# A graph network with two layers: the store of a block's counts asked for at the top of SyncE's turn

## The chip, the cores and the metric

The kernel runs on one core of a Trainium2 chip. The metric is the device time of one execution in microseconds (us). Five engines with instruction streams of their own take part: TensorE (PE, with its weight loads as PEld), VectorE (DVE), ScalarE (ACT), GpSimd (POOL) and SyncE (SP), which here only asks for DMAs. They meet at semaphores alone.

## What is computed

There are 6250 nodes with 128 features each and 200000 edges, sorted by the node they end at. Cut to what matters:

```python
h = x @ W + b_W;  xi, xj = split(h)
xji = (xj[src] + edge_attr @ W_e + b_We) / (in_degree[dst] + 1e-6)
x1 = layernorm(x + xi + segment_sum(xji, dst))
h2 = x1 @ W1                                 # with self loops and degree norm
out = segment_sum(h2[src] * norm, dst) + b1
y = leaky_relu(batchnorm(out) * gamma + beta)
result = layernorm(x1 + y)
```

## The kernel before

**Blocks and turns.** The nodes are worked through in 25 blocks of 256. For each block the kernel builds a table of counts (how many edges go from each source node to each node of the block) as products of one-hot matrices, 16 slots to a block. A sum over edges is then a matrix product with the table. Each engine runs a loop of turns `b` that are written out in full. In turn `b`, slot `s`, these are the steps that matter here:

- VectorE builds the one-hot matrices of two slots at a time (`one_hots`, L608 to L622), in a ring of six slots that TensorE's counting frees. At slot 2 it makes the keys of the next block (`make_keys`) and the edge keys of the one before (`edge_keys`, which need the loaded destinations).
- TensorE counts a slot (`count`, L852, products of L858), which waits until ScalarE has emptied the slot before the last (`pair_out` of slot s-2), for there are two buffers `pair_ps`. Then it does a fifteenth of the product of the block before with its table (`product`, L863, products of L876 and L884), and at two slots the sums of 4 streams of edge rows (`edges`, L895).
- ScalarE casts each counted slot into the table in SBUF (`pair_out`, L1056, cast of L1065). There are two tables, `counts[b % 2]`, so at slot 0 it first waits until the table of block b-2 is in HBM (L1061, semaphore `counts_kept`). At slot 10 it waits for a load of 64.5 KB of destinations, `rows_i`, and turns them into floats for block b+4 (`float_rows(b + 4)`, L1144 to L1153, called at L1183). Its instructions run in order, so whatever stands behind one of these waits is held up too.
- SyncE asks for DMAs (L398 to L425): the row load for block b+4 (`load_rows`, L299), eight register loads of start values (`start_values`, L325), the eight small loads of edge destinations (`load_destinations`, L330), the inverse degrees (`keep_inverse`), then the store of the counts of block b-1 (`keep_counts(b - 1)`, L346), which waits for the block's last cast, then early sums, four loads of 576 KB of edge rows (`load_edges(b, 0)`, L336), the store of finished rows (`keep_rows(b - 2)`, L357, which waits for ScalarE's slot 12), and four more loads of edge rows.

After the last block the tables are loaded again for the second layer (L426 to L441), and a last stage normalises and writes the rows.

**What sets the order around the change.** All of SyncE's DMAs go to one hardware queue, in the order in which its instructions stand. The store is 3136 KB for blocks 0 and 1 and gets smaller, down to 1600 KB, because part of a later block's table is used at once for the second layer and need not be kept. Blocks 23 and 24 are not stored.

Of the kernel before, what the change touches and what calls it, by code (L numbers as in the profile page):

```python
# [31 lines left out]
NB = -(-N // BN)  # L32
# [47 lines left out]
def slots(b):  # L80
    return SL if b < NB - 1 else LAST_SLOTS


def first_slot(b):
    return SL * b
# [6 lines left out]
def cols(b):  # L92
    return 2 * SW * slots(b)
# [15 lines left out]
def groups(b):  # L109
    return 2 if b < NB - 1 else -(-LAST // (EG * EC))  # L110
# [13 lines left out]
def early(k):  # L124
    return min(4 * max(0, k - 1), EARLY_MOST)
# [69 lines left out]
def layers(nc, block, x, src, dst, ea, W0, b0, We, be, keep, scratch):  # L195
    with ExitStack() as ctx:
# [102 lines left out]
        def load_rows(engine, b):  # L299
            reach(engine, S["rows_float"], b - ROW_RING + 1)  # L300
            engine.dma_start(rows_i[b % ROW_RING][:, :],
                             bass.AP(tensor=dst.tensor, offset=first_row(b), ap=[[HR, P], [1, HR + 1]]))\
                  .then_inc(rows_in[b % ROW_RING], 16)

        def load_late_rows(engine):
            engine.wait_ge(S["late_cleared"], 1)
            at = E - ROW_SPAN
            engine.dma_start(late_rows_i[0:P - 1, :],
                             bass.AP(tensor=dst.tensor, offset=at, ap=[[HR, P - 1], [1, HR + 1]])).then_inc(S["late_rows_in"], 16)
            engine.dma_start(late_rows_i[P - 1:P, 0:HR], dst[E - HR:E].rearrange("(o n) -> o n", o=1))\  # L310
                  .then_inc(S["late_rows_in"], 16)

        @block.sync
        def _(sp):
# [10 lines left out]
            def start_values(b):  # L325
                sp.wait_ge(S["starts_known"], b + 1)
                return [sp.value_load(estart_i[EP * c:EP * c + 1, b:b + 1], min_val=0, max_val=E - EE)
                        for c in range(groups(b) * EG)]

            def load_destinations(b, starts):  # L330
                reach(sp, S["e_keyed"], b - 1)
                for c in range(groups(b) * EG):
                    sp.dma_start(edst[b % 2][:, c, :], dst[bass.ds(starts[c], EE)].rearrange("(p j) -> p j", j=EJ))\
                      .then_inc(edst_in[b % 2], 16)

            def load_edges(b, g, starts):  # L336
                reach(sp, S["e_summed"], edge_group(b - 1, g) + 1)
                if b == 0 and g == 1:
                    sp.wait_ge(S["x_low"], len(X_PIECES))
                    sp.wait_ge(S["x_turned"], len(OWN))  # L340
                for c in range(EG):
                    sp.dma_start(ebuf[g][:, c, :, :].rearrange("p j f -> p (j f)"),
                                 ea[bass.ds(starts[g * EG + c], EE), :].rearrange("(p j) f -> p (j f)", j=EJ))\
                      .then_inc(e_in[g], 16)

            def keep_counts(k):  # L346
                sp.wait_ge(S["pair_out"], first_slot(k) + slots(k))
                at, n = early(k) // 2 * cols(k), HS * cols(k)
                sp.dma_start(scratch["counts"][k * P:(k + 1) * P, at:n], counts[k % 2][:, at:n])\
                  .then_inc(counts_kept[k % 2], 16)  # L350

            def keep_early(k):
                sp.wait_ge(S["early_out"], early_blocks(k + 1))
                n = cols(k)
                sp.dma_start(scratch["sz"][:, k * BN:k * BN + n], early_sum[k % 2][:, 0:n]).then_inc(early_kept[k % 2], 16)

            def keep_rows(u):  # L357
                sp.wait_ge(S["x1_ready"], u + 1)
                if u < NB - 1:
                    sp.dma_start(scratch["x1"][u * BN:u * BN + BN, :].rearrange("(p t) f -> p t f", t=2),  # L360
                                 x1[u % 2][:, :, :]).then_inc(x1_kept[u % 2], 16)
                    return
                for half in range(2):
                    sp.dma_start(scratch["x1"][u * BN:N, :].rearrange("(p t) f -> t p f", t=2)[half],
                                 x1[u % 2][64 * half:64 * half + LAST_P, 0, :]).then_inc(x1_kept[u % 2], 16)

            def keep_inverse(b):
                sp.wait_ge(S["shares_ready"], b + 1)
                n = P if b < NB - 1 else 64
                sp.dma_start(scratch["dinv"][b * BN:b * BN + 2 * n].rearrange("(p t) -> p t", t=2),  # L370
                             dinv[0:n, 2 * b:2 * b + 2]).then_inc(S["dinv_kept"], 16)

            def load_counts(i):
                b = AGAIN[i]
                at, n = early(b) // 2 * cols(b), HS * cols(b)
                if i < 4:
                    sp.wait_ge(S["e_summed"], edge_group(NB - 1, groups(NB - 1) - 1) + 1)
                else:
                    sp.wait_ge(S["z_gathered"], i - 3)
                sp.wait_ge(counts_kept[b % 2], 16 * (b // 2 + 1))  # L380
                sp.dma_start(again[AGAIN_AT[i % 4]][:, at:n], scratch["counts"][b * P:(b + 1) * P, at:n])\
                  .then_inc(counts_in[i % 4], 16)
# [14 lines left out]

            for b in range(NB + 2):  # L398
                u = b - 2
                if b + ROW_RING < LATE:  # L400
                    load_rows(sp, b + ROW_RING)
                if b + ROW_RING == LATE:
                    load_late_rows(sp)
                if b < NB:
                    starts = start_values(b)
                    load_destinations(b, starts)
                    keep_inverse(b)
                if 1 <= b <= NB - 2:
                    keep_counts(b - 1)
                if early(b - 2):  # L410
                    keep_early(b - 2)
                if b == NB:
                    sp.dma_start(w1[:, :], keep["W1"]).then_inc(S["vectors_in"], 16)
                    for k, a in enumerate(keep["vectors1"]):
                        sp.dma_start(vec[:, k:k + 1], a.rearrange("(p o) -> p o", o=1)).then_inc(S["vectors_in"], 16)
                    sp.wait_ge(S["dinv_kept"], 16 * NB)
                if b < NB:
                    load_edges(b, 0, starts)
                if 0 <= u < NB:
                    keep_rows(u)  # L420
                if b < NB and groups(b) > 1:
                    load_edges(b, 1, starts)
                if b == NB - 1:
                    load_counts(0)
                    load_counts(3)  # L425
# [425 lines left out]
        def _(pe):  # L851
# [111 lines left out]
            def turn_x(m):  # L963
                h, n = OWN[m]
                piece = [h < 2 * z for _, z in X_PIECES].index(True)
                last_piece = [h + n <= 2 * z for _, z in X_PIECES].index(True)
                for k in range(piece, last_piece + 1):
                    pe.wait_ge(S["x_in"][k], 16 * x_loads(k))
                pe.wait_ge(S["consts"], CONSTS)
                reach(pe, S["xT_out"], m - 1)  # L970
                for k in range(n):
                    last = nc.tensor.transpose(turn_ps[m % 2][:, k, :], xrows[:, h + k, :], ident[:, :])
                last.then_inc(S["x_turned"], 1)
# [832 lines left out]
```

## Time and profile before

| | before |
|---|---|
| median of 3 runs | 938.35 us (937.87 to 938.45) |
| the profiled execution, its own time | 936.68 us |
| its span, first to last instruction | 934.6 us |
| mean granted TensorE clock | 0.985 |
| busy: PE, DVE, ACT, POOL | 95%, 72%, 48%, 37% of the span |
| q1, SyncE's DMA queue | 239.46 MB, 73.7% of 16 engines' span |

The profile is one execution of the program. Times in its rows count from the first instruction. A row of the timeline gives the start, the length, the engine (SPq is SyncE's sequencer, which asks for DMAs), the line, the operation with what it writes and reads, how many instructions are merged, and in brackets the idle time of the engine before it with what ended it.

### The profile page before, as it was taken

Reading aid. Unit: us, or ns where it says so; the run is one execution under the profiler, and the core shown is the slowest. Engines: PE = TensorE matmul, PEld = TensorE weight load, DVE = VectorE, ACT = ScalarE, POOL = GpSimd, SP = SyncE. Lnnn points to the kernel's source line nnn. Section 1 sums busy time; section 2 is a strip of 40 time slices with the busy share of each in tenths; the row PEclk is TensorE's granted clock in tenths of the full one; section 3 lists DMA queues with packets and bytes.
Section 4 is the critical chain, followed back from the end, with each engine's and each line's share of the span. In section 5 each row is a group of like instructions: output and inputs, shape, how many; then the busy total and the mean of one; then the engine's idle time right before and its main releaser. Section 6 shows DMA issues by size and latency. Waiting matters only on the chain.

```text
span 934.6 us, 30500 instructions
## 1 busy us (share of the span) xinstructions
PE 883.9 (95%) x12210; PEld 791.2 (85%) x12210; DVE 676.6 (72%) x1249; ACT 450.3 (48%) x983; POOL 349.4 (37%) x401
## 2 busy tenths in 40 slices
PE   4867999999999999999999999999999999999995
PEld 4756888888988898989899999999988888888874
DVE  6999899999999998899888899888842111112255
ACT  3764666656666665556565556565542000000026
POOL 2236444455554444455334455434332011112200
PEclk8988999999999999999999999999999999999998
DMA  6428999998879788777878758678667897779654
GB/s 180 110 83 296 361 345 320 317 342 290 313 247 319 284 311 283 229 229 241 253 264 277 223 185 301 214 274 282 209 216 299 343 358 279 272 260 326 249 155 136
DMA packets 96762, 244.77 MB, mean 262 GB/s; under 512 B 39560, under 2 KB 64838, under 8 KB 90726
## 3 DMA queue, kind: packets, MB, share of 16 engines
q1 hardware_dynamic: 95014, 239.46, 73.7%
q0 software_dynamic: 1600, 3.28, 1.4%
q8 instruction: 100, 1.64, 0.8%
q14 instruction: 48, 0.39, 0.2%
HBM read 183.85 MB, written 58.85 MB: 260 GB/s over the span
## 4 chain that ended last, share of the span: by engine, by line
PE 85%; DVE 5%; issue 3%; ACT 3%; DMA 1%; SPq 1%; ACTq 0%; DVEq 0%
PE x_ps L876 26%; PE pair_ps L951 19%; PE pair_ps L858 13%; PE e_ps L895 10%; PE x_ps L884 9%; PE j_ps L933 2%; PE j_ps L981 2%; DVE lo_oh L616 1%; DVE key_oh L619 1%; PE pair_ps L960 1%; PE j_ps L934 1%; ACT counts L1065 1%; PE u_vps L1409 1%; DMA counts_kept<-counts 1%; DMA streams<-in_x 1%
## 5 line engine op out<-in xcount | busy, mean ns | idle before, releaser
L1065 ACT CAST counts<-pair_ps 128x784 bf16<-128x784 f32 x391 | 315.3, 817 | 251.5 <-PE pair_ps L858 244.1
L876 PE MATMUL x_ps<-counts,xsplit 128*128 128x256 bf16 (+1 forms) x2450 | 307.5, 271 | 0.0
L616 DVE TENSOR_TENSOR lo_oh<-counter,lo_t 128x2048 bf16<-128x2048 bf16 x196 | 252.3, 1287 | 53.9 <-PE pair_ps L858 52.5
L876 PEld LDWEIGHTS x_ps<-counts,xsplit 128*128 128x128 f16 x2450 | 222.1, 98 | 29.3 <-issue 7.1
L858 PE MATMUL pair_ps<-key_oh,lo_oh 128*128 128x100 bf16 x3128 | 207.8, 209 | 22.5 <-ACT counts L1065 15.4
L858 PEld LDWEIGHTS pair_ps<-key_oh,lo_oh 128*128 128x128 bf16 x3128 | 182.8, 98 | 36.9 <-issue 15.0
L619 DVE TENSOR_TENSOR key_oh<-counter,key_t 128x1600 bf16<-128x1600 bf16 x196 | 196.4, 1002 | 0.0
L895 PE MATMUL e_ps<-streams 128*32 128x128 f32 x3528 | 106.9, 274 | 0.1
L884 PE MATMUL x_ps<-counts,zown 128*128 128x256 bf16 (+1 forms) x840 | 105.9, 269 | 0.1
L951 PE MATMUL pair_ps<-streams,zown 128*128 128x256 bf16 x878 | 99.0, 273 | 0.0
L895 PEld LDWEIGHTS e_ps<-streams 128*32 128x32 f32 x3528 | 93.3, 110 | 4.8 <-issue 1.0
L476 POOL TENSOR_SCALAR quot<-deg 128x2 f32<-128x2 f32 x25 | 5.7, 226 | 243.2 <-DVE junk L595 231.5
L951 PEld LDWEIGHTS pair_ps<-streams,zown 128*128 128x128 f16 x878 | 85.8, 98 | 11.4 <-issue 0.2
L884 PEld LDWEIGHTS x_ps<-counts,zown 128*128 128x128 f16 x840 | 76.1, 97 | 10.3 <-issue 2.9
L492 POOL TENSOR_SCALAR bias<-linear,share 128x128 f32<-128x128 f32 x50 | 76.0, 1532 | 14.7 <-DVE vo L705 13.7
L951 PE MATMUL pair_ps<-counts,zown 128*128 128x256 bf16 (+1 forms) x732 | 79.9, 268 | 0.0
L951 PEld LDWEIGHTS pair_ps<-counts,zown 128*128 128x128 f16 x732 | 69.3, 98 | 9.2
L1313 ACT ACTIVATE u_co<-u_co 128x1 f32<-128x1 f32 x1 | 0.2, 203 | 156.0 <-DVEq L1351 156.0
L825 DVE TENSOR_TENSOR s_mem<-pair_ps,key_oh 128x256 f32<-128x256 f32 (+1 forms) x23 | 9.6, 418 | 83.8 <-PE pair_ps L951 81.3
L639 DVE TENSOR_TENSOR streams<-iota,ekeys 128x1152 f32<-128x1152 f32 x49 | 67.5, 1377 | 2.7 <-PE e_ps L895 0.3
L833 DVE TENSOR_TENSOR xsplit<-pair_ps,key_oh 128x256 f32<-128x256 f32 (+1 forms) x25 | 10.5, 419 | 58.7 <-PE pair_ps L960 57.0
L507 POOL TENSOR_TENSOR streams<-streams,key_oh 128x512 bf16<-128x512 bf16 x13 | 15.0, 1151 | 84.9 <-DMA streams<-counts_kept 84.9
(181 smaller groups left out, 890.6 us busy)
## 6 DMA issues: line engine op xcount, KB each, us to landing
streams<-in_edge_attr SPq DMA_DIRECT2D x196, 576.0 KB, 9.1
counts_kept<-counts SPq DMA_DIRECT2D x10, 1600.0 KB, 9.1
streams<-counts_kept SPq DMA_DIRECT2D x6, 1600.0 KB, 6.5
counts<-counts_kept SPq DMA_DIRECT2D x4, 1600.0 KB, 7.1
counts_kept<-counts SPq DMA_DIRECT2D x2, 3136.0 KB, 12.7
streams<-counts_kept SPq DMA_DIRECT2D x2, 3136.0 KB, 14.8
edst<-in_dst SPq DMA_DIRECT2D x196, 4.5 KB
streams<-in_x SPq DMA_DIRECT2D x3, 1024.0 KB, 5.7
```

What stands on the lines that cost most here:

```text
L492: last = g.tensor_scalar(bias[:, t, :], bje, share[:, 2 * b + t:2 * b + t + 1], None, ALU.mult)
L616: dv.tensor_tensor(lo_oh[:, ring, :, :, :].rearrange("p r w k t -> p (r w) k t"), counter[:, :, :].unsqueeze(1).to_broadcast([P, g, P, 2]) ...
L619: dv.tensor_tensor(key_oh[:, ring, :, :, :].rearrange("p r w k t -> p (r w) k t"), counter[:, 0:KW, :].unsqueeze(1).to_broadcast([P, g, KW ...
L639: dv.tensor_tensor(e_oh[g][:, :, :], iota[:, 0:EC].unsqueeze(1).to_broadcast([P, EG * EJ, EC]), ekeys[:, k].unsqueeze(2).to_broadcast([P, ...
L858: last = nc.tensor.matmul(pair_ps[at % 2][:, half_of, col:col + KW], lo_oh[:, at % RING, w // 2, :, w % 2], key_oh[:, at % RING, w // 2, : ...
L876: last = nc.tensor.matmul(x_ps[:, 0, 0:n], xsplit[:, q // 2, q % 2, :], by_hi[:, q // 2, :], start=(q == 0), stop=(q == 2 * HS - 1))
L884: last = nc.tensor.matmul(x_ps[:, 1, 0:n], zsplit[:, z // 2, z % 2, :], by_hi[:, z // 2, :], start=(z == 0), stop=(z == early(k) - 1))
L895: last = nc.tensor.matmul(e_ps[EC * c:EC * (c + 1), g, :], e_oh[g][:, c * EJ + j, :], ebuf[g][:, c, j, :], start=(j == 0), stop=(j == EJ - 1))
L933: nc.tensor.matmul(out, sx[:, t:m:2], wj, start=True, stop=False)
L951: last = nc.tensor.matmul(z_ps[i % 2][:, 0:n], zsplit[:, q // 2, q % 2, :], by_hi[:, q // 2, :], start=(q == early(b)), stop=(q == 2 * HS ...
L981: last = nc.tensor.matmul(j_ps[:, k, :], xT[m % 2][:, k, :], wi, start=True, stop=True)
L1065: a.copy(out.rearrange("p h (g n) -> p h g n", g=2), pair_ps[at % 2][:, :, 0:4 * KW].rearrange("p g (n h) -> p h g n", h=HI)[:, 0:HS]).the ...
```

## The change

One call is moved within SyncE's turn. Nothing is added or removed; the DMAs, their sizes and the semaphores stay the same.

```diff
             for b in range(NB + 2):
                 u = b - 2
+                if 1 <= b <= NB - 2:
+                    keep_counts(b - 1)
                 if b + ROW_RING < LATE:
                     load_rows(sp, b + ROW_RING)
                 if b + ROW_RING == LATE:
@@
                     starts = start_values(b)
                     load_destinations(b, starts)
                     keep_inverse(b)
-                if 1 <= b <= NB - 2:
-                    keep_counts(b - 1)
                 if early(b - 2):
                     keep_early(b - 2)
```

## Rows read from the trace of the kernel before

**Rows 1.** The page, part 1: busy time of TensorE.

```profile
PE 883.9 (95%) x12210; PEld 791.2 (85%) x12210; DVE 676.6 (72%) x1249; ACT 450.3 (48%) x983; POOL 349.4 (37%) x401
```

**Rows 2.** Waits of PE from 112 to 700 us: total, times, longest.

```profile
PE pair_ps L858 <- ACT counts L1065: 4.5, 11, 0.6
```

**Rows 3.** Timeline of ScalarE, 72.6 to 94.5 us (turn 1 into turn 2).

```profile
73.34 0.30 ACT L1151 ACTIVATE heads<-rows_i,shift 128x2 f32<-128x2 int32 x1
...
73.83 0.80 ACT L1065 CAST counts<-pair_ps 128x784 bf16<-128x784 f32 x1
...
81.69 0.49 ACT L1073 ACTIVATE sx<-x_ps,xscale 128x256 f32<-128x256 f32 x1
87.80 1.53 ACT L1065 CAST counts<-pair_ps 128x784 bf16<-128x784 f32 x2 [5.61 <-issue]
```

**Rows 4.** Timeline of SyncE, 63 to 90 us (its turn 1).

```profile
65.69 0.44 SPq L301 DMA_DIRECT2D rows_i<-in_dst  x1
71.10 3.85 SPq L333 DMA_DIRECT2D edst<-in_dst  x8
...
75.47 0.43 SPq L349 DMA_DIRECT2D counts_kept<-counts  x1
76.10 6.77 SPq L342 DMA_DIRECT2D streams<-in_edge_attr  x8
```

**Rows 5.** DMAs asked at 65.28, 65.69, 75.47, 76.10 us; last column: us to landing.

```profile
streams<-in_edge_attr SPq DMA_DIRECT2D x1, 576.0 KB, 7.7
rows_i<-in_dst SPq DMA_DIRECT2D x1, 64.5 KB, 7.5
...
counts_kept<-counts SPq DMA_DIRECT2D x1, 3136.0 KB, 12.3
...
streams<-in_edge_attr SPq DMA_DIRECT2D x1, 576.0 KB, 13.1
```

**Rows 6.** Timeline of PE, 77.6 to 95 us.

```profile
77.66 0.53 PE L858 MATMUL pair_ps<-key_oh,lo_oh 128*128 128x100 bf16 x8
...
78.79 0.53 PE L858 MATMUL pair_ps<-key_oh,lo_oh 128*128 128x100 bf16 x8
...
83.28 0.93 PE L876 MATMUL x_ps<-counts,xsplit 128*128 128x256 bf16 x7
88.75 0.83 PE L858 MATMUL pair_ps<-key_oh,lo_oh 128*128 128x100 bf16 x8 [4.55 <-ACT counts L1065]
...
93.88 0.93 PE L876 MATMUL x_ps<-counts,xsplit 128*128 128x256 bf16 x7
```

**Rows 7.** Busy time by stretch, 88 to 92 us: PE, PEld, DVE, ACT, POOL, PEclk, DMA, GB/s.

```profile
88.00:92.00 4.00, 3.25 (x27) 2.84 (x28) 3.92 (x8) 2.46 (x5) 2.37 (x5) 0.50 1.03 413
```

**Rows 8.** Timeline of ScalarE, 48 to 58 us: the last two casts of block 0.

```profile
51.66 1.53 ACT L1065 CAST counts<-pair_ps 128x784 bf16<-128x784 f32 x2
```

**Rows 9.** Timeline of ScalarE, 341 to 345 us: last cast of block 11.

```profile
341.98 0.81 ACT L1065 CAST counts<-pair_ps 128x784 bf16<-128x784 f32 x1 [0.60 <-PE pair_ps L858]
```

**Rows 10.** Timeline of SyncE, 338 to 356 us (its turn 12).

```profile
341.56 0.43 SPq L301 DMA_DIRECT2D rows_i<-in_dst  x1
...
353.80 0.43 SPq L349 DMA_DIRECT2D counts_kept<-counts  x1
```

**Rows 11.** Waits of SyncE's sequencer, whole span: total, times, longest.

```profile
SPq L360 <- ACT x_mem L1106: 167.2, 23, 9.3
```

**Rows 12.** Waits of DVE from 52 to 115 us: total, times, longest.

```profile
DVE lo_oh L616 <- PE pair_ps L858: 2.7, 3, 2.1
DVE row_junk L569 <- ACT lo_t L1090: 1.4, 1, 1.4
```

**Rows 13.** Busy time from 112 to 208 us, columns as in rows 7.

```profile
112.00:208.00 96.00, 92.31 (x1517) 82.83 (x1518) 94.43 (x168) 61.53 (x127) 50.77 (x56) 1.00 0.94 333
```

**Rows 14.** Timeline of ScalarE, 103 to 105 us: slot 10 of turn 2.

```profile
103.77 0.30 ACT L1151 ACTIVATE heads<-rows_i,shift 128x2 f32<-128x2 int32 x1
```

**Rows 15.** The page, part 6: the last ten stores of counts.

```profile
counts_kept<-counts SPq DMA_DIRECT2D x10, 1600.0 KB, 9.1
```

## The prediction

> **What bounds the kernel now.** I read the page's first part, then the waits of TensorE, then the chain around the first store. TensorE is busy for 95% of the span [rows 1]. From 112 to 700 us, which covers turns 3 to 24, its longest kind of wait adds up to 4.5 us in 11 waits of at most 0.6 us [rows 2]. So from turn 3 on nothing that SyncE does earlier can win anything, and whatever TensorE loses before 112 us stays lost. What matters lies in turns 1 and 2.
>
> There the timeline of ScalarE has one large hole: after the cast for the first product at 81.69 it sits idle for 5.61 us and casts slot 0 of block 2 only at 87.80 [rows 3]. The trace names no releaser ("issue"), but the code does: L1061 waits there for the store of block 0, whose table is to be overwritten. SyncE asked for that store at 75.47 [rows 4] and it landed 12.3 us later [rows 5], at 87.8. TensorE stood still for 4.55 us because of it [rows 6] and came back at a granted clock of 0.50, its 1.2 GHz level [rows 7]. This is the stall that the earlier store aims at.
>
> **The change, part by part.**
>
> *The store in turn 1 is asked for earlier.* SyncE is at the top of turn 1 at 65.69 [rows 4]. The last cast of block 0 ended at 51.66 + 1.53 = 53.2 [rows 8], so the moved wait costs nothing here and the store is asked for at 65.7 instead of 75.47.
>
> *When it lands.* The queue is not empty: the last of four edge loads was asked for at 65.28 and landed 7.7 us later, at 73.0; the row load, asked for next, landed at 65.69 + 7.5 = 73.2, just behind it [rows 5]. And an edge load asked for at 76.10, 0.6 us behind the store, took 13.1 us and landed at 89.2, which is 1.4 us after the store [rows 5]. So DMAs of this queue land in the order in which they were asked for. The store took 12.3 us from an empty queue. Some 2 us of that is start-up: 576 KB took 1.4 us behind other work, and 3136 KB at that pace are 7.8 us, but the store writes to HBM and may be slower. I take 10.3 us of service, near the row of the store itself, with 7.8 and 12.3 as ends. It then lands at 73.0 + 10.3 = 83.3 (80.8 to 85.3).
>
> *What is pushed behind it.* Moved past it are the row load, eight register reads, eight destination loads and the inverse degrees. The row load now stands behind 3136 KB. It lands 0.2 us behind the store, as it did behind the edge load, at 83.5 (81.0 to 85.5) instead of 73.2. ScalarE wants it in slot 10 of the same turn, at 73.34 [rows 3]: today it arrives just in time. So ScalarE will stand in `float_rows(5)` for 83.5 - 73.3 = 10.2 us, with the last five casts of turn 1 queued behind. The old stall of 5.61 us is gone (when slot 0 of block 2 comes, the store has landed), and a longer one stands in its place, some 8 us earlier.
>
> *What TensorE loses.* Its count of slot 13 needs the cast that follows the floats. Today that cast ends at 73.83 + 0.80 = 74.6 and the count starts at 77.66 [rows 3, 6], so 3.0 us of delay are free. After: floats at 83.5, cast from 84.0 to 84.8, count at 85.0. That is 85.0 - 77.66 = 7.3 us of delay. From there TensorE today needs until 83.28 + 0.93 = 84.2 to reach its hole, and leaves it at 88.75, 11.1 us after 77.66 [rows 6]. After, the same work without the hole takes 11.1 - 4.55 = 6.5 us, so that it is there at 91.5, which is 2.8 us later than 88.75.
>
> *The clock.* Today the work from 88.75 to 93.88 takes 5.1 us [rows 6]. At the pace of two counts 1.13 us apart (77.66, 78.79) it would take 2.9 with its three short key products, so the low clock [rows 7] costs 2.2 us. After, TensorE is idle longer, 7 us instead of 4.55, and comes back at 85.0, so the same cost falls due, and more of the slow stretch may be spent at work: between 0 and 1.6 us more (2.2 for 5.1 us, times the 3.7 us by which it starts earlier). I take 0.6.
>
> *Sum:* -4.55 (hole gone) + 7.3 (new hole) + 0.6 (clock) = +3.4 us, rounded. The ends of the landing (81.0 and 85.5) and of the clock give +0.3 to +6.4.
>
> *Can it be given back?* VectorE's ring is six slots. While TensorE stands, VectorE fills it and stands too, until slot 13 is counted at 85.5. In turn 2 it has 2.7 + 1.4 = 4.1 us of idle time today [rows 12], in which it catches up. From 112 to 208 us VectorE is busy for 94.4 of 96 us and TensorE for 92.3 [rows 13], and after that TensorE is the bound, so nothing returns the 3.4 us.
>
> *Turn 2.* The store of block 1 now waits for the last cast, at 83.5 + 8.4 = 91.9 or earlier (today 81.69 - 73.34 = 8.4 us hold all that is left of the turn [rows 3]). The row load follows it, where today it was asked for before. Ahead of both stand eight edge loads of 1.4 us, from 83.7 to about 95; the store to 105.6; the rows at 105.8. They are wanted at 103.77 + 3.4 = 107.2 [rows 14], with 3.0 us free behind that. No stall, with a margin of some 4 us.
>
> *Turns 3 to 23.* SyncE reaches the top of turn 12 at 341.56, and the block's last cast ends at 341.98 + 0.81 = 342.8 [rows 9, 10]. So the moved wait costs SyncE 1.2 us, the store is asked for some 11 us earlier than 353.80 [rows 10], and all that is moved behind it is a little over 1 us later. SyncE's own spare time covers that: it waits 167.2 us in 23 turns for finished rows [rows 11], 7.3 in each. The row load again stands behind a store, but this shrinks to 1600 KB, 9.1 us [rows 15]. Cost 0 while that cover lasts; if it goes, it is the third case below.
>
> The Trainium skill has a rule that speaks for another outcome. In "DMA: Bandwidth & Descriptors", section "Queues, rings and completion order", it says that descriptors of a ring are taken in order but without a barrier, so a later one may finish its write before an earlier one. By that rule the rows could overtake the store, and the sum would be that of the first rival instead of +3.4. The trace does not agree at this size: the edge load behind a store landed after it [rows 5].
>
> Against the runs: the profiled execution took 936.68 us, 1.67 less than the median of 938.35. I put the difference on the median: 938.35 + 3.4 = 941.8.
>
> **Rivals.**
>
> *1. Faster: the row load does not wait for the store.* Then only the old stall goes. VectorE then sets the pace of turn 2, which can shorten by VectorE's idle time at most, 4.1 us [rows 12]: 934.3. It decides if the rows land by about 76.2 (73.2 today and the 3.0 free). Against it stand the landings of rows 5; for it, that all of them are large loads or stand behind loads, except one. 0.13.
>
> *2. No change.* The two stalls weigh the same if the new one is 3 us shorter, with the rows landing at 80 to 81, for instance because the store's service is nearer 7.8 us. Or the clock comes back sooner. 938.4. The 12.3 us of the row speak against it. 0.13.
>
> *3. Slower still: the rows come late in later turns too.* From turn 2 to about turn 5 the stores are near 3 MB and stand behind edge loads. If gathers from GpSimd, which share the engines, push the landings 5 us past my reckoning, ScalarE stands in slot 10 again, at 1 to 2 us a turn: three turns, +4, so 945.8. 0.12.
>
> *The forecast*, one stall moved and made longer: 0.62.
>
> **How the numbers follow.** About 0.2% (1.9 us) is what a measurement of this kernel can tell from no change. Slower by more is the forecast (0.62, of which 0.03 falls short of 1.9 us) and rival 3: 0.62 - 0.03 + 0.12 = 0.71. Same: 0.13 + 0.03 = 0.16. Faster: 0.13. The forecast with its unknown costs spans 938.7 to 944.8. The range 938.0 to 945.0 holds it, some two thirds of rival 2 and a third of rival 3, about 0.75 to 0.8.
>
> **What would show it.** In turn 1 the store is asked for at 65.7 and the rows at 66.2, and these land near 83.5. ScalarE has an idle time of about 10 us ahead of the floats of L1151, ended by the row load, and none of 5.6 us ahead of the first cast of turn 2. TensorE has a hole of about 7 us from 77.8 to 85, with the clock at 0.50 behind it. In turn 12 the store is asked for within 2 us of the last cast. The prediction is wrong if the rows land before 80, if there is no idle time ahead of L1151 in turn 1, or if it comes back in turn 2 and later.

## The result, and the profile after

The change makes the kernel slower: 952.02 us against 938.11, medians of six runs each, a ratio of 1.0159 (95% interval 1.0118 to 1.02). That is 14 us, beyond the forecast's 941.8 and beyond its range. The runs of after spread over 10 us (948.86 to 958.99), those of before over 4. The profiled execution of after took 956.96 us, so its trace shows some 5 us more than the median.

The page of after, first the span, the busy times (against [rows 1]), then one of its DMA queues (packets, MB, share of 16 engines):

```profile
span 955.0 us, 30500 instructions
...
PE 890.3 (93%) x12210; PEld 794.6 (83%) x12210; DVE 677.7 (71%) x1249; ACT 450.9 (47%) x983; POOL 351.5 (37%) x401
...
q8 instruction: 100, 1.64, 0.7%
```

TensorE is busy for 6.4 us more with the same 12210 products, and the span is 20.4 us longer. The extra time is thus partly idle time, partly products that take longer.

**Where the 20.4 us lie.** I cut both traces at the end of the last cast of a block (ScalarE, L1065): a turn starts there. The table gives the length of each stretch in us.

| stretch | before | after | more |
|---|---|---|---|
| start to turn 1 | 53.2 | 54.9 | 1.7 |
| turns 1 and 2 | 58.8 | 62.9 | 4.1 |
| turns 3 to 10 | 204.4 | 217.0 | 12.6 |
| turns 11 to 23 | 361.9 | 363.9 | 2.0 |
| the rest | 256.4 | 256.3 | -0.1 |

The first row is no effect of the change: it lies ahead of the first moved store and reads 53.2 to 54.9 in all the kernels run here. Turns 1 and 2 are what the forecast spoke of. Turns 3 to 10 are where it put nothing.

**Turn 1.** The timeline of SyncE in after, against [rows 4]:

```profile
67.50 0.45 SPq L349 DMA_DIRECT2D counts_kept<-counts  x1
67.99 0.47 SPq L301 DMA_DIRECT2D rows_i<-in_dst  x1
```

The timeline of ScalarE in after, against [rows 3]:

```profile
74.32 0.81 ACT L1065 CAST counts<-pair_ps 128x784 bf16<-128x784 f32 x1 [0.37 <-issue]
87.35 0.30 ACT L1151 ACTIVATE heads<-rows_i,shift 128x2 f32<-128x2 int32 x1 [12.22 <-DMA rows_i<-in_dst]
...
94.81 1.54 ACT L1065 CAST counts<-pair_ps 128x784 bf16<-128x784 f32 x2
```

And the timeline of TensorE in after, against [rows 6]:

```profile
78.59 0.92 PE L876 MATMUL x_ps<-counts,xsplit 128*128 128x256 bf16 x7
88.78 0.82 PE L858 MATMUL pair_ps<-key_oh,lo_oh 128*128 128x100 bf16 x8 [9.27 <-ACT counts L1065]
```

The row load was asked for behind the store and came 19.4 us later (67.99 to 87.35). ScalarE stood 12.22 us for it, and TensorE 9.27 us for ScalarE. The cast at 94.81, the first of block 2, has no idle time ahead of it: the 5.61 us of [rows 3] are gone, and more than twice as much stands a few us earlier.

**Turns 3 to 10.** Busy time by stretch for the same stretch of the program (3208 products in each), first of before, columns as in [rows 7]:

```profile
112.00:316.30 204.30, 198.93 (x3208) 179.80 (x3208) 196.00 (x357) 132.24 (x272) 101.55 (x112) 1.00 0.90 318
```

and of after:

```profile
117.80:334.80 217.00, 203.79 (x3208) 182.57 (x3208) 196.39 (x357) 132.59 (x273) 102.23 (x112) 0.98 0.88 293
```

TensorE's idle time grew from 204.3 - 198.9 = 5.4 us to 217.0 - 203.8 = 13.2, which is 7.8 more, and its busy time by 4.9 us, at a mean granted clock of 0.98 instead of 1.00. Together these are the 12.6 us. The waits of TensorE from 112 to 700 us say which idle time grew, against [rows 2] (total, times, longest):

```profile
PE pair_ps L858 <- issue: 5.1, 2, 3.5
PE pair_ps L858 <- ACT counts L1065: 4.7, 11, 0.6
PE e_ps L895 <- issue: 4.1, 5, 1.7
PE x_ps L884 <- issue: 1.1, 2, 0.9
```

The wait for ScalarE is the same (4.5 us before, 4.7 now). New are nine stops without a releaser, 10.3 us in all. In before this view has one line of that kind:

```profile
PE pair_ps L858 <- issue: 1.2, 1, 1.2
```

**What these stops are.** The longest one, in the timeline of TensorE of after:

```profile
217.40 0.48 PE L858 MATMUL pair_ps<-key_oh,lo_oh 128*128 128x100 bf16 x7
221.33 0.22 PE L858 MATMUL pair_ps<-key_oh,lo_oh 128*128 128x100 bf16 x1 [3.45 <-issue]
```

and the one of before:

```profile
205.72 0.48 PE L858 MATMUL pair_ps<-key_oh,lo_oh 128*128 128x100 bf16 x7
207.45 0.22 PE L858 MATMUL pair_ps<-key_oh,lo_oh 128*128 128x100 bf16 x1 [1.24 <-issue]
```

It is the same place in both: between the seventh and the eighth product of one slot's eight, where the program has no wait at all. So TensorE did not wait for data. Now the products between one stop of after and the next, as busy time by stretch of TensorE alone (length, busy, number of products, granted clock, DMA share, GB/s); each stretch begins and ends at the first product behind a stop:

```profile
128.37:168.74 40.37, 38.49 (x623) 1.00 0.98 303
168.74:193.74 25.00, 24.12 (x373) 0.93 0.88 315
193.74:204.79 11.05, 9.66 (x121) 1.00 0.99 332
204.79:221.33 16.54, 13.09 (x252) 1.00 0.85 266
221.33:289.18 67.85, 65.89 (x993) 0.97 0.86 293
289.18:305.00 15.82, 14.94 (x252) 1.00 0.72 211
305.00:566.12 261.12, 258.44 (x3982) 1.00 0.81 259
```

The counts are 5, 3, 1, 2, 8, 2 and 32 times a number between 121 and 126; the longest gives 3982 / 32 = 124.4. The stops lie on a grid of 124.4 products, or, as each product has a weight load, of some 249 instructions. And the page's queue q8, whose kind is "instruction", moved 1.64 MB in 100 packets of 16.4 KB: 24420 instructions of TensorE / 100 = 244 in each. So a stop falls where one 16 KB packet of TensorE's own program ends and the next has to be there. The DMA view of after for three stretches around the stop of 3.45 us (packets, MB, share of 16 engines), in order: 210 to 219, 219 to 220, 220 to 221.3 us:

```profile
q1 hardware_dynamic: 1317, 1.56, 73.3%
...
q1 hardware_dynamic: 75, 0.32, 92.5%
q8 instruction: 1, 0.02, 6.1%
...
q1 hardware_dynamic: 131, 0.54, 103.1%
```

For nine us no packet of instructions came; one came between 219 and 220, and the product ran at 221.33. The same view, taken from each stop of after to the next, has 5, 3, 1, 2, 8, 2 and 32 packets of q8, one for each step of the grid. Here are the stretches 221.33 to 289.18 and 305.00 to 566.12:

```profile
q8 instruction: 8, 0.13, 0.7%
...
q8 instruction: 32, 0.52, 0.8%
```

It holds for all the kernels below too: the thirteen traces have 51 such stops from 112 to 700 us, and ahead of 50 of them a packet of q8 had landed 1.2 to 1.6 us before the product ran. In ten of the thirteen the same product, the one at 221.33 in after and at 207.45 in before, stands behind a stop.

Two of the stops are paid twice, for the clock falls behind them:

```profile
170.00:174.00 4.00, 3.83 (x23) 3.25 (x24) 4.00 (x6) 2.34 (x5) 3.75 (x4) 0.59 1.02 418
222.00:226.00 4.00, 4.00 (x33) 3.29 (x32) 2.54 (x5) 2.96 (x8) 0.00 (x0) 0.58 0.49 136
```

Behind the stops of 1.66 us (at 168.74) and of 3.45 us (at 221.33) TensorE runs mostly at the 1.2 GHz level. The length of a stop alone does not decide it: behind the one of 1.75 us that ends at 128.38 the clock stays at 1.00 (first line of the stretches above). The stretches between stops show it as 0.93 over 25.0 us and 0.97 over 67.85, which is some 1.75 + 2.0 = 3.8 of the 4.9 us of longer products.

The Trainium skill describes this traffic in "Runtime: NRT & Kernel Launch", section "Instruction fetch mechanics": an engine's instructions are refilled in blocks of 16 KiB, 256 instructions, over a DMA queue that the sequencer drives itself, and the cost of crossing a block is mostly hidden. The trace agrees on the block (249 counted, besides those that the count of products and weight loads leaves out). It agrees on "mostly hidden" for before, with 1.2 us between 112 and 700 us, and not for after, with 10.3.

**What fills the engines there.** The busy share of the 16 DMA engines in turn 3, in 40 slices of 0.7 us, 112 to 140 us of before:

```profile
DMA  9999999999999646790109939994959999999999
```

and 117.8 to 146 us of after:

```profile
DMA  9999899989999999799789999399276999999999
```

In before SyncE asks for the store at 122.22, as the edge loads of the turn before come to their end, and the engines have slices of 0 and 1 in the middle of the turn. In after it asks at 117.95, the store follows those edge loads at once, and most of the gap is filled. An estimate, which places the first product of each 16 KB block by counting products between the stops, shows the packets falling back: in turns 3 to 10 a packet begins to move, on average, 3.3 us after TensorE has entered the block ahead of it in before, and 4.8 us after that in after. The stop that ends at 128.38 lies 10 us behind this store; the one that ends at 168.74 lies 10 us behind the first of the turn's next edge loads, asked for at 158.63.

### The profile page after: what moved, and what is told of

It is laid out like the page before. It is cut to its first block, busy times and chain, and to the rows that moved or that the text cites. A ratio compares the mean times of both kernels' runs of the same rounds, so it can differ in the third digit from the quotient of the medians.

```text
span 955.0 us, 30500 instructions
## 1 busy us (share of the span) xinstructions
PE 890.3 (93%) x12210; PEld 794.6 (83%) x12210; DVE 677.7 (71%) x1249; ACT 450.9 (47%) x983; POOL 351.5 (37%) x401
## 3 DMA queue, kind: packets, MB, share of 16 engines
q8 instruction: 100, 1.64, 0.7%
## 4 chain that ended last, share of the span: by engine, by line
PE 87%; issue 3%; DVE 3%; ACT 3%; DMA 3%; SPq 0%; ACTq 0%; DVEq 0%
PE x_ps L876 26%; PE pair_ps L951 18%; PE pair_ps L858 14%; PE e_ps L895 11%; PE x_ps L884 9%; DMA rows_i<-in_dst 2%; PE j_ps L933 2%; PE j_ps L981 2%; PE j_ps L934 1%; ACT counts L1065 1%; PE pair_ps L960 1%; PE u_vps L1409 1%; DMA streams<-in_x 1%; ACT u_xo L1328 1%; PE e_ps L903 1%
## 5 line engine op out<-in xcount | busy, mean ns | idle before, releaser
L1065 ACT CAST counts<-pair_ps 128x784 bf16<-128x784 f32 x391 | 314.7, 817 | 256.9 <-PE pair_ps L858 249.7
L619 DVE TENSOR_TENSOR key_oh<-counter,key_t 128x1600 bf16<-128x1600 bf16 x196 | 198.7, 1014 | 0.0
L895 PE MATMUL e_ps<-streams 128*32 128x128 f32 x3528 | 109.0, 274 | 4.2 <-issue 4.1
L895 PEld LDWEIGHTS e_ps<-streams 128*32 128x32 f32 x3528 | 94.0, 110 | 10.2 <-issue 6.4
L492 POOL TENSOR_SCALAR bias<-linear,share 128x128 f32<-128x128 f32 x50 | 73.2, 1475 | 14.6 <-DVE vo L705 13.7
L833 DVE TENSOR_TENSOR xsplit<-pair_ps,key_oh 128x256 f32<-128x256 f32 (+1 forms) x25 | 10.5, 419 | 58.8 <-PE pair_ps L960 56.9
```

The costliest lines, as they stand in the source:

```text
L492: last = g.tensor_scalar(bias[:, t, :], bje, share[:, 2 * b + t:2 * b + t + 1], None, ALU.mult)
L619: dv.tensor_tensor(key_oh[:, ring, :, :, :].rearrange("p r w k t -> p (r w) k t"), counter[:, 0:KW, :].unsqueeze(1).to_broadcast([P, g, KW ...
L895: last = nc.tensor.matmul(e_ps[EC * c:EC * (c + 1), g, :], e_oh[g][:, c * EJ + j, :], ebuf[g][:, c, j, :], start=(j == 0), stop=(j == EJ - 1))
L1065: a.copy(out.rearrange("p h (g n) -> p h g n", g=2), pair_ps[at % 2][:, :, 0:4 * KW].rearrange("p g (n h) -> p h g n", h=HI)[:, 0:HS]).the ...
```

## The experiments

Eleven runs, of ten kernels, were made in four batches, each beside runs of the kernel before on the same chip (medians 937.05, 937.37, 937.68 and 938.41 us). A ratio is to the runs of before in the same batch. Theory A puts the whole loss on turn 1: the row load behind the store. Theory B says that turn 1 costs what was forecast, and that the rest is lost in the later turns by the early store as such.

**Turn 1 alone.**

```diff
+                if b == 1:
+                    keep_counts(b - 1)
                 if b + ROW_RING < LATE:
                     load_rows(sp, b + ROW_RING)
...
-                if 1 <= b <= NB - 2:
+                if 2 <= b <= NB - 2:
                     keep_counts(b - 1)
```

> Only the store of block 0 (turn 1) is asked for at the top of the turn; the stores of turns 2 to 23 stay where they were. Theory A (the row load waits behind the store, and that is the whole cost): ScalarE stands some 12 us ahead of the floats of turn 1 and the time is that of the change, 949 to 953. Theory B (the row load in turn 1 costs 4 to 5 us; the rest is TensorE running out of instructions in turns 3 to 10, because its instruction loads compete with a store that now runs while the first edge sums eat instructions fastest): the same hole in turn 1, but no idle times inside groups of products later, and 942 to 943.

Measured: 942.22 us, 1.0051 (1.0033 to 1.0069). Theory A falls. ScalarE's timeline has the forecast's stall:

```profile
82.81 0.30 ACT L1153 ACTIVATE heads<-rows_i,shift 128x2 f32<-128x2 int32 x1 [8.90 <-DMA rows_i<-in_dst]
```

So the mechanism that was forecast costs 5.2 us (3.1 to 6.5 by the interval), and not 14.

**All but turns 1 and 2.**

```diff
+                if 3 <= b <= NB - 2:
+                    keep_counts(b - 1)
                 if b + ROW_RING < LATE:
...
-                if 1 <= b <= NB - 2:
+                if 1 <= b <= 2:
                     keep_counts(b - 1)
```

> The stores of turns 3 to 23 are asked for at the top, those of turns 1 and 2 where they were. Theory A: no hole in turn 1 and so no cost, 937 to 939. Theory B: turn 1 as before, but TensorE stops inside groups of products in turns 3 to 10 with nothing to wait for, 8 to 10 us with the low clock behind it: 945 to 948.

Measured: 947.79 us, 1.0126 (1.0089 to 1.0163), in the range of theory B. But its trace shows two things at work, and so the number agrees in part by luck. The row load is late in two later turns, by 2.28 us at 185.51 and most in turn 3 (timeline of ScalarE):

```profile
134.22 0.30 ACT L1153 ACTIVATE heads<-rows_i,shift 128x2 f32<-128x2 int32 x1 [6.22 <-DMA rows_i<-in_dst]
```

and the waits of TensorE from 112 to 700 us hold the wait for ScalarE that follows from it, with the longer stops beside it:

```profile
PE pair_ps L860 <- ACT counts L1067: 7.6, 11, 3.3
PE e_ps L897 <- issue: 1.7, 3, 0.8
PE x_ps L886 <- issue: 1.3, 1, 1.3
```

The stops come to 3.6 us in six, not to the 8 to 10 expected. The wait of 3.3 us is the one in turn 3, and behind it the clock is at 0.50 from 135.65 to 141 us. Turns 3 to 10 are 8.6 us longer than in before, and the larger part of that is the late row load and this clock. So this run does not tell the two causes apart; the next pair does.

**The row load out of the way, in all turns and in turn 1.** In the first kernel the store stays at the top of every turn but behind the row load; in the second this is done in turn 1 alone, and the other stores are where they stood before.

```diff
                 if b + ROW_RING == LATE:
                     load_late_rows(sp)
+                if 1 <= b <= NB - 2:
+                    keep_counts(b - 1)
                 if b < NB:
...
-                if 1 <= b <= NB - 2:
-                    keep_counts(b - 1)
```

> The store stands at the top of every turn but behind the row load, so that the rows don't wait for it. Theory A: the hole in turn 1 goes, the old one of 5.6 us in turn 2 shrinks to 1 or 2 us, and the time falls to about 934, below the kernel before. Theory B: the same in turns 1 and 2, but the stops of turns 3 to 10 stay: 934 + 9, 940 to 946.

```diff
+                if b == 1:
+                    keep_counts(b - 1)
                 if b < NB:
...
-                if 1 <= b <= NB - 2:
+                if 2 <= b <= NB - 2:
                     keep_counts(b - 1)
```

> Only the store of turn 1 is moved up, to a place behind the row load; all others as before. Both theories: the stall of 5.6 us at the start of turn 2 shrinks to 1 or 2 us, with no hole in turn 1 and no stops later: about 934, faster than the kernel before by 0.4%.

Measured: 946.15 us, 1.0099 (1.0063 to 1.0135), and 935.68 us, 0.9986 (0.9971 to 1.0001). They differ only in the early stores of turns 2 to 23, and these cost 10.5 us though no row load stands behind one. From turn 3 to turn 23 the profiled executions differ by 11.1 us: 7.6 of idle time of TensorE and 3.5 of longer products. The waits of TensorE in the first, from 112 to 700 us, have 8.7 us of stops in seven where the second has 1.5 in one:

```profile
PE x_ps L876 <- issue: 2.6, 1, 2.6
PE e_ps L895 <- issue: 2.3, 2, 1.4
PE pair_ps L858 <- issue: 2.2, 2, 2.1
...
PE x_ps L884 <- issue: 1.6, 2, 0.9
```

In the second, ScalarE's old stall of 5.61 us [rows 3] shrank to 3.46 us, not to the 1 to 2 that I had reckoned, and the rows came in time:

```profile
75.35 0.30 ACT L1153 ACTIVATE heads<-rows_i,shift 128x2 f32<-128x2 int32 x1 [0.39 <-DMA rows_i<-in_dst]
...
87.25 2.34 ACT L1067 CAST counts<-pair_ps 128x784 bf16<-128x784 f32 x3 [3.46 <-issue]
```

Part of the gain is given back in the turns that follow. VectorE waits for a gather, and TensorE from 112 to 700 us waits for VectorE (waits of VectorE from 52 to 115 us, then of TensorE):

```profile
DVE bit_i L584 <- DMA gsrc<-in_src,start_i: 2.3, 1, 2.3
...
PE pair_ps L860 <- DVE key_oh L621: 1.6, 2, 0.9
PE pair_ps L860 <- issue: 1.5, 1, 1.5
```

The stops of the first lie on the grid of after. Its products between three of its stops (columns as above), and the timeline of its stop at 208.81:

```profile
183.58:208.82 25.24, 22.49 (x374) 1.00 0.96 317
208.80:276.14 67.34, 65.47 (x994) 0.97 0.88 294
...
208.81 0.22 PE L858 MATMUL pair_ps<-key_oh,lo_oh 128*128 128x100 bf16 x1 [2.07 <-issue]
```

374 is what lies between 193.74 and 221.33 in after (121 + 252), 994 what lies between 221.33 and 289.18, give or take a product at the ends. Another kernel, other times, the same places in the program: a wait for a load of data would move with the loads.

**Is it the size of a store's pieces or the amount that is under way?** Two forms of theory B. B1: the store's 25 KB rows hold up whatever comes behind them in a DMA engine, and smaller rows would help. B2: it is the unbroken backlog of store and edge loads. The first kernel below is the one with the row load first and each store asked for as four DMAs of a quarter of the columns (and the waits for stores counted accordingly). The second is the same kernel as it was, but the first four edge loads of a turn, from block 2 on, bring one of nine rows in each partition; the rest of those edge rows is left out.

```diff
+                part = (n - at) // 4
+                for q in range(at, n, part):
+                    sp.dma_start(scratch["counts"][k * P:(k + 1) * P, q:q + part], counts[k % 2][:, q:q + part])\
+                      .then_inc(counts_kept[k % 2], 16)
```

> As e3_rows_first, but each store is asked for in four DMAs of a quarter of its columns, so that a row of a partition goes in pieces of 6.3 KB and less instead of 25 KB. Theory B1 (TensorE's instruction load is held up by the large pieces of the store in its DMA engine): the stops of turns 2 to 10 mostly go, 935 to 939. Theory B2 (it is held up by whatever transfer is in flight while it is wanted, whatever the size of its pieces): no change against e3, 944 to 948.

```diff
+                if b >= 2 and g == 0:
+                    for c in range(EG):
+                        sp.dma_start(ebuf[g][:, c, 0, :],
+                                     ea[bass.ds(starts[g * EG + c], EE), :].rearrange("(p j) f -> p (j f)", j=EJ)[:, 0:F])\
+                          .then_inc(e_in[g], 16)
+                    return
```

> As e3_rows_first, but from turn 2 on each of the first four edge loads of a turn brings one of nine rows (64 KB instead of 576 KB); the other eight rows are left out, so that after the store, when TensorE's second burst of edge products comes, nothing large is in flight. Theory B2: the stops near the second burst (20 to 25 us after the turn's start) go, those near the first burst (8 to 10 us, store in flight) stay: 938 to 942. Theory B1: the store is what counts, so it stays at 943 to 948. Theory A': it is not the instruction loads but something that the move does to ScalarE or SyncE: unchanged, 944 to 948.

Measured: 943.91 us, 1.0074 (1.0047 to 1.0101), and 939.75 us, 1.0021 (1.0008 to 1.0034). The first interval overlaps that of the undivided store (1.0063 to 1.0135): B1 is not supported, but a part of it is not excluded, for the trace of the divided store, its fastest run, has 4.5 us of stops in five where the undivided store has 8.7. The second takes away most of the loss, as B2 said. Theory A', that the move does something to ScalarE or SyncE, gave 944 to 948 for the second and is out. In the trace of the second (936.6 us, the fastest of its ten runs) two stops are left from 112 us on, each some 8 us behind the store of its turn (asked for at 111.88 and 136.22), which is still under way; those in the second burst of edge loads are gone (timeline of TensorE):

```profile
120.91 0.43 PE L901 MATMUL e_ps<-streams 128*32 128x128 f32 x8 [0.93 <-issue]
...
145.65 1.06 PE L901 MATMUL e_ps<-streams 128*32 128x128 f32 x27 [1.15 <-issue]
```

The control has the same small edge loads with the stores of turns 2 to 23 in their old place:

```diff
+                if b == 1:
+                    keep_counts(b - 1)
...
-                if 1 <= b <= NB - 2:
+                if 2 <= b <= NB - 2:
```

> The control for e6_small_edges: the same small first edge loads from turn 2 on (one of nine rows, the other eight left out), but the stores of turns 2 to 23 in their old place, as in e4_turn1_rows_first. Theory B2: the one stop of 1.5 us that e4 still has near a second burst goes too, since nothing large is behind the store then: 933 to 936. Against e6 it is faster by the stops of the first burst, 2 to 4 us. If the small loads win time in another way, it is below 932.

Measured: 937.02 us, 1.0 (0.9985 to 1.0014), a us above what I had expected; its trace keeps two stops, 1.3 us. With small edge loads the early stores cost 939.75 - 937.02 = 2.7 us (2.0 by the ratios, which is fairer, as the two ran in different batches), where they cost 10.5 with whole ones.

The converse leaves the edge loads whole and makes the stores small: with the row load first, the stores of blocks 1 to 22 write an eighth of their columns, and the second layer reads the table of block 0 in place of the others.

```diff
+                n = n if k == 0 else at + (n - at) // 8
...
-                sp.dma_start(again[AGAIN_AT[i % 4]][:, at:n], scratch["counts"][b * P:(b + 1) * P, at:n])\
+                sp.dma_start(again[AGAIN_AT[i % 4]][:, at:n], scratch["counts"][0:P, at:n])\
```

> As e3_rows_first, but the stores of blocks 1 to 22 write one eighth of their columns (the rest is left out, and the second layer loads the table of block 0 for every block in its place). The early store is then short, and the first edge loads behind it run from an empty queue. Theory B2: no stops near the first burst, and few near the second, since the edge loads have mostly landed by then: 935 to 939. Theory A' (something that the move does to ScalarE or SyncE, not the transfer): 944 to 948 as in e3.

Measured: 939.4 us, 1.0013 (0.9998 to 1.0028). So neither of the two does it alone: taking the bulk out of either removes most of the 9 us of the kernel with the row load first. Its trace still has 4.2 us of stops in five. It has no control with small stores in the old place, so what small stores win by themselves is not known.

**The store half-way.** Between the reading of the start values and the destinations; the rest as before.

```diff
                     starts = start_values(b)
+                    if 1 <= b <= NB - 2:
+                        keep_counts(b - 1)
                     load_destinations(b, starts)
```

> The store stands half-way: behind the row load and the start values, ahead of the destinations, some 5 us earlier than in the kernel before. Rows don't wait for it. Theory B2: the store is in flight during the first burst, the edge loads behind it land a few us earlier than before, so some of the stops come: 939 to 945. If only the place behind the edge loads at the very top costs: 935 to 938.

Measured: 945.37 us, 1.0062 (1.0039 to 1.0086; its runs reach from 941.84 to 947.0), just above the range of B2. That place costs as well: in turn 3 the store is asked for at 118.61 us, while the edge loads of the turn before are still arriving. The waits of its TensorE from 112 to 700 us have 7.9 us of stops in six, the longest 2.4 us.

**Early stores in late turns only.** Row load first, for turn 1 and for turns 11 to 23, whose stores are smaller.

```diff
+                if b == 1 or 11 <= b <= NB - 2:
+                    keep_counts(b - 1)
...
-                if 1 <= b <= NB - 2:
+                if 2 <= b <= 10:
```

> As e4_turn1_rows_first, and the stores of turns 11 to 23, 2 MB and less, are moved up behind the row load too. Theory B2 by the trace of the change, which shows almost no stops from turn 11 on: no cost, 935 to 938. If every early store costs alike (10.5 us in 22 turns): 6 us for 13 turns, 941 to 943.

Measured: 939.71 us, 1.0027 (1.0012 to 1.0042), which falls between the two expectations. The profiled execution shows 1.8 us of stops and 2.1 us more in the second layer, so where the 4 us against the kernel that moves turn 1 alone come from stays open.

**The best version, five rounds.** The kernel with turn 1's store alone moved, behind the row load:

> The kernel of e4_turn1_rows_first, timed in five rounds, because its interval took in no change. By e4: 0.9986 of the kernel before, 935.7, clear of 1 in this longer comparison. If the shorter stall at the start of turn 2 is wholly given back by VectorE's pace in turns 3 to 5: 0.999 to 1.001, 937 to 938.

Measured: 936.31 us against 938.41, 0.9981 (0.997 to 0.9992): faster than the kernel before by some 2 us (0.8 to 2.8 by the interval), as expected.

## Why the prediction was wrong

It was right in direction, and its mechanism is there; it was wrong in size, by a step that it put at nothing.

- *The store in turn 1, and the row load behind it.* Right. The rows came 19.4 us behind their request in after (16.0 in the kernel with turn 1 alone) where 83.5 - 66.2 = 17.3 was forecast, and ScalarE stood 12.22 and 8.90 us where 10.2 was. Rival 1, a row load that does not wait, is out.
- *The hole of TensorE and the clock.* Right in kind: 9.27 us in after and 5.18 in the kernel with turn 1 alone, against 7.3, at a clock of 0.50 behind it.
- *The sum, +3.4 us.* It stands for turn 1: the kernel that has this alone measured +5.2 (3.1 to 6.5), and turns 1 and 2 of after show +4.1. As its hole was shorter than forecast and its cost was not, the agreement is in part luck.
- *Turn 2.* Nearly right: the margin of some 4 us was not there, and ScalarE waited 0.49 us for its rows at 110.21.
- *Turn 12.* Right: the block's last cast ends at 360.70 + 0.81 = 361.51, and the store is asked for 0.03 us later (timelines of ScalarE and SyncE):

```profile
360.70 0.81 ACT L1065 CAST counts<-pair_ps 128x784 bf16<-128x784 f32 x1 [0.60 <-PE pair_ps L858]
...
361.54 0.33 SPq L349 DMA_DIRECT2D counts_kept<-counts  x1
```

- *"Turns 3 to 23 ... Cost 0 while that cover lasts."* This is the step that failed. It asked who waits for the moved requests, SyncE and the row load, and found spare time for both. It did not ask who else uses the DMA engines. The early stores in turns 2 to 23 cost 10.5 us (the pair that differs in them alone), because TensorE's instructions come over the same engines and arrive late in an unbroken backlog: 8.7 us of stops against 1.5. The sentence "from turn 3 on nothing that SyncE does earlier can win anything" speaks of winning, and I let it stand for "can lose anything". The trace of before had a sign of it, the stop of 1.24 us inside a group of eight products, in the same view as [rows 2]; I read only the wait for ScalarE there.
- *Rival 3, rows late in later turns.* It occurs: 8.5 us in two waits in the kernel that starts with turn 3, where it makes the larger part of the loss, and 2.3 us in three waits in after from 92 to 700 us. But it is a small part of after, where TensorE's wait for ScalarE did not grow, and the kernel with the row load first loses 9 us without it.
- *The bound of rival 1.* Not tested. In the kernel with turn 1's store alone, behind the row load, the store still held ScalarE for 3.46 of the old 5.61 us; TensorE's hole shrank from 4.55 to 2.39 us, and some 2 us were won. What the whole 4.55 would bring stays open.

Shown are the places of the stops (the grid, alike in several kernels), the packet of instructions that lands just ahead of 50 of 51, and that less data under way takes most of the loss away. Only argued is the step between: in what order a DMA engine serves the queues, and so why a 16 KB packet is held up for as long as it is.

## What to carry to other kernels

A kernel whose loops are written out in full streams its own program over the DMA engines that carry its data: before moving a large transfer forward, look whether it closes a gap in which TensorE's instructions used to arrive, and what the gap between bursts was worth. Idle time named "issue" inside a group of products that has no wait is the sign; count the products between two such stops, and if they lie on a grid of a fixed number, with a packet of the instruction queue landing just ahead of each, it is the program that was late. And where one store holds up one engine once, move that one store, behind the small loads that are wanted soon.

## What was not expected

TensorE uses up a packet of instructions with each 124.4 products, in the long stretch above one in 261.12 / 32 = 8.2 us, and a queue that stands at 0.7% of the engines' span in the page set some 10 us of the kernel's time. A stop of 1.66 us in an otherwise busy stretch was followed by a slower clock that cost about as much again (1.75 us), and one of 1.75 us was not. And cutting the store's rows from 25 KB to 6.3 KB made no difference outside the interval.
